# Scattering the first mixture's weighted results back to the tokens, with eight weight staging buffers in place of two

## What is computed

```python
# 1. first mixture of experts: 8 experts and 2 shared ones, 2 of the 8 for each token
topk_w, topk_idx = top_k(softmax((x @ wt.T + repeat(cond @ wg.T)) / 2), 2)   # weights divided by their sum
gp = leaky(einsum('th,ehm->etm', x, w_gate)); up = einsum('th,ehm->etm', x, w_up)
y_all = einsum('etm,emh->eth', gp * up, w_down)
y = sum over the 2 chosen experts of topk_w * y_all  +  shared(x)
# 2. attention with a relative bias over each sequence; x = x + attention(y)
# 3. a second attention, with mask, null key and normalizations
# 4. second mixture: 64 experts, 8 for each token, and a shared one; x = x + mixture(...)
```

## Time and profile before

| | us |
|---|---|
| median of 3 runs | 1968.0 (1967.81 to 1972.55) |
| the profiled execution, its own time | 1952.01 |
| its span, first to last instruction | 1950.0 |
| first mixture, to the first transfer of the attention | 0 to 307.6 |
| first attention, its slots 0 to 31 | 333.5 to about 650 |
| TensorE busy in the span | 75% |
| VectorE, ACT, GpSimd busy | 58%, 41%, 50% |

### The profile page before, as it was taken

One profiled execution on the slowest core, in us unless ns is written; L12 is line 12 of the kernel. 1 busy time (PEld: TensorE's weight loads), 2 busy tenths in 40 slices (PEclk: granted clock), 3 DMA queues, 4 the chain that ended last, 5 costly groups with the idle time before them and its releaser, 6 DMA issues. The chain is left out here.

```text
span 1950.0 us, 34468 instructions
## 1 busy us (share of the span) xinstructions
PE 1462.8 (75%) x11604; PEld 1158.4 (59%) x11605; DVE 1137.3 (58%) x2661; ACT 807.9 (41%) x1567; POOL 967.2 (50%) x888
## 2 busy tenths in 40 slices
PE   6955975576768799999999998520877877787771
PEld 4645973354445476776776776310776767676671
DVE  6633662577776546878778779630333355555555
ACT  2322431333343345655655645410444444454440
POOL 2572143665654211255555555663455555656562
PEclk9977987888889899999999999865988888888885
DMA  9553658455565000011111111636444577777755
GB/s 340 168 189 106 198 155 249 114 142 159 166 170 155 23 2 2 17 61 56 56 56 56 63 58 56 262 137 196 150 137 149 170 219 238 238 240 234 220 157 162
DMA packets 193490, 278.87 MB, mean 143 GB/s; under 512 B 27722, under 2 KB 161489, under 8 KB 190934
## 3 DMA queue, kind: packets, MB, share of 16 engines
q1 hardware_dynamic: 145030, 150.76, 26.7%
q0 software_dynamic: 33792, 84.23, 12.3%
q10 hardware_dynamic: 14544, 42.21, 6.9%
HBM read 133.38 MB, written 152.11 MB: 146 GB/s over the span
## 5 line engine op out<-in xcount | busy, mean ns | idle before, releaser
L2290 POOL DMA_INDIRECT y_rows<-se_ys,se_yidx x320 | 327.5, 1023 | 253.8 <-issue 217.1
L1461 POOL DMA_INDIRECT x_slots<-wide,a_sidx x256 | 259.6, 1014 | 85.6 <-issue 71.6
L2323 PE MATMUL ps<-se_xsT,se_up 128*128 128x128 f32 x1280 | 206.1, 329 | 93.9 <-DVE se_hT L2414 92.6
L2323 PEld LDWEIGHTS ps<-se_xsT,se_up 128*128 128x128 f32 x1280 | 194.1, 240 | 102.2 <-issue 81.4
L1450 POOL TENSOR_TENSOR flat<-flat,a_rs 128x512 f32<-128x512 f32 x64 | 69.9, 1092 | 268.3 <-DVE a_rs L1943 268.3
L2414 DVE SCALAR_TENSOR_TENSOR se_hT<-ps,se_hT 128x512 f32<-128x512 f32 x80 | 55.3, 691 | 212.1 <-ACT se_hT L2364 201.3
L2312 PE MATMUL ps<-ident,se_xs 128*128 128x128 f32 x640 | 86.3, 279 | 113.1 <-DMA se_xs<-x_slots 95.9
L2335 PE MATMUL ps<-wide,se_hT 128*128 x640 | 162.5, 399 | 1.7 <-ACT se_ys L2370 1.7
L2312 PEld LDWEIGHTS ps<-ident,se_xs 128*128 128x128 f32 x640 | 75.5, 144 | 126.7 <-issue 112.0
L2356 ACT COPY se_up<-w_up 128x256 f32 x320 | 106.9, 405 | 104.5 <-issue 100.7
L2335 PEld LDWEIGHTS ps<-wide,se_hT 128*128 128x128 f32 x640 | 125.2, 207 | 18.3 <-issue 3.3
(11 more groups left out here) (339 smaller groups left out, 3535.3 us busy)
## 6 DMA issues: line engine op xcount, KB each, us to landing
x_slots<-wide SPq DMA_DIRECT2D x40, 1032.0 KB, 13.8
se_xs<-x_slots SPq DMA_DIRECT2D x80, 516.0 KB
se_got<-y_rows ACTq DMA_DIRECT2D x64, 512.0 KB
x_slots<-wide SPq DMA_DIRECT2D x10, 1024.0 KB, 11.3
wide<-x_slots SPq DMA_DIRECT2D x20, 512.0 KB
y_slots<-wide SPq DMA_DIRECT2D x20, 512.0 KB
w_up<-in_up SPq DMA_DIRECT2D x8, 1024.0 KB
y_rows<-se_ys,se_yidx POOLq DMA_INDIRECT x320
```

Of the source, the lines that this page charges most:

```text
L1461: pool.indirect_dma_start(out=x_slots, out_offset=bass.IndirectOffsetOnAxis(ap=sidx[:, r % 2, t, k_:k_ + 1], axis=0), in_=stage[:, t, k_, ...
L2290: pool.indirect_dma_start(out=y_rows, out_offset=bass.IndirectOffsetOnAxis(ap=yidx[:, (w - 2) % TR, b:b + 1], axis=0), in_=ys[:, w % 2, b, ...
L2323: last = pe.matmul(ps[:, 2, b * P:(b + 1) * P], up[:, (w - 1) % 2, b, c, :], xsT[:, (w - 1) % 2, b, c, :], start=(c == 0), stop=(c == C - 1))
```

## The change

- Slots of the first mixture become rows of 258 numbers. `xr` holds each tile twice (one copy for each of the two experts), GpSimd writes place and weight behind the features, and scatters quarters of a half (`send`): 8 indirect DMAs, in four quarters for each half. `xr` holds two quarters, so SP loads quarter q (`load_rows`) when quarter q-2 has landed in DRAM, and all eight such loads now stand in SP's queue ahead of the first group's load.
- Evictions of a group multiply by the weight out of `xs` (two operations of 256 columns on each of ACT and VectorE where there was one of 512), and GpSimd scatters the four blocks of each group to the tokens' rows `y1_rows` (4 indirect DMAs a group, 80 in all). The store by SP, and 64 gathers, are gone.
- The rows of a group stay in `xs` until its scatter has landed; `xs` has five places, `ys` three. Group g is loaded when the scatter of group g-5 has landed.
- The two returned rows of each token are added unweighted, four tiles at a time: SP loads them (`load_returned` for the first half; one load in each of the blocks 0 to 3 of the attention for the second) and VectorE adds (two operations of 1024 columns). In the attention the adds stand in slots 4, 9, 13 and 17, and SP waits for the one before at each of its blocks.
- Staging has eight places, six of them in the part of `acc` that is written last. Eight experts load ahead of the rows of x; ACT rounds all of these before block 0 and the last two at its end; GpSimd makes all ten rests before its first scatter.
- TensorE loads ten packed words of four expert numbers once for each half (`table`) and works out the places with register arithmetic.

```diff
+        YR = 3
...
+                XS = 5
+                xs = wide[:, 0:XS * GB * ROW].rearrange("p (w b d) -> p w b d", w=XS, b=GB)
+                XR1 = 8
+                xr = sb("xr", [P, XR1, K1, ROW])
...
                     load_features(0)
-                    load_expert(0)
-                    load_expert(1)
-                    load_rows(0, 0)
-                    load_rows(0, 1)
-                    sp.wait_ge(pad_step, 1)
+                    for q in range(N1 - 2):
+                        load_expert(q)
+                    load_rows(0)
+                    load_rows(1)
+                    sp.wait_ge(pad_step, 2)
                     clear_slots(0)
+                    load_expert(N1 - 2)
+                    load_expert(N1 - 1)
                     load_features(1)
...
+                    for q in range(4, NB):
+                        load_rows(q)
                     for dst, src in ((wq, wqT), (wk, wkT), (wv, wvT), (wo, woT)):
...
                         wait(sp, t_ps, g - 1)
-                        sp.dma_start(xs[:, g % 2], xv[g // GPB][g % GPB]).then_inc(xs_in[g % 2], 16)
+                        if g >= XS:
+                            sp.wait_ge(y1_out[(g - XS) % YR], returned((g - XS) % YR, g - XS + 1))
+                        sp.dma_start(xs[:, g % XS], xv[g // GPB][g % GPB]).then_inc(xs_in[g % 2], 16)
+                    for g in range(NG1):
+                        load_slots(g)
+                        if NG1 - 4 <= g < NG1 - 2:
+                            load_returned(g - (NG1 - 4))
+                    load_returned(2)
+                    load_returned(3)
...
+                    for g in range(NG1):
+                        pool.wait_ge(ya_done, NB + g + 1)
+                        pool.wait_ge(yb_done, g + 1)
+                        for b in range(GB):
+                            pool.indirect_dma_start(
+                                out=y1_rows[g // GPB],
+                                out_offset=bass.IndirectOffsetOnAxis(ap=xs[:, g % XS, b, D:D + 1].bitcast(I32), axis=0),
+                                in_=ys[g % YR][:, b, :], in_offset=None, bounds_check=TB * P * K1 - 1, oob_is_err=False
+                                ).then_inc(y1_out[g % YR], 16)
...
+                    def table(beta):
+                        pe.wait_ge(be_ready, beta + 1)
+                        pe.load(regs[beta], be_i[0:1, beta * GPB:(beta + 1) * GPB])
...
-                            act.copy(ys[:, g % 2, 0:2, :].rearrange("p b d -> p (b d)"), ps[:, 4, :]).then_inc(ya_done, 1)
+                            for b in range(2):
+                                last = act.activation(ys[g % YR][:, b, :], ps[:, 4, b * D:(b + 1) * D], ACT.Copy,
+                                                      scale=xs[:, g % XS, b, D + 1:ROW])
...
             def sync_program(sp):
...
                     sp.dma_start(xres[:, b % 2], xv[:, b * TPB:(b + 1) * TPB, :]).then_inc(res_in[b % 2], 16)
+                    if b < 4:
+                        sp.wait_ge(added1, 4 + b)
+                        sp.dma_start(got, y1_tiles[1][:, b * TPB:(b + 1) * TPB]).then_inc(got1_in[0], 16)
                     for g in range(b * fills, (b + 1) * fills):
...
-            GATHER_AT = [2 + j + j // TPB for j in range(TB)]
+            RETURNED_AT = [4, 9, 13, 17]
```

More of the change, by code:

```diff
@@ L175, in build, with returned @@
         WIDE = 2 * C * M1 + D
[L176 to L182, removed]
+        YR = 3
+        x1_slots = [nc.dram_tensor(f"x1_slots{beta}", (EB * P, ROW), F32).ap() for beta in range(2)]
+        y1_rows = [nc.dram_tensor(f"y1_rows{beta}", (TB * P * K1, D), F32).ap() for beta in range(2)]
+        y1_tiles = [rows.rearrange("(t p k) d -> p t k d", p=P, k=K1) for rows in y1_rows]
+        y1_out = [sem(f"y1_out{w}") for w in range(YR)]
+        got1_in, added1 = [sem("got1_in0"), sem("got1_in1")], sem("added1")
+        def returned(w, groups):
+            return len(range(w, groups, YR)) * GB * 16
         def first_experts():
@@ L396, in _ @@
[L396 to L405 removed]
+                        pool.tensor_tensor(wl[:, ORDER[q], :], wf[q], wh[:, ORDER[q], :], ALU.subtract).then_inc(wl_ready, 1)
@@ L581, in _ @@
                     features(0)
-                    features(1)
                     weights(0)
                     weights(1)
+                    features(1)
+                    for q in range(2, 6):
+                        weights(q)
                     exponential(0)
+                    weights(6)
+                    weights(7)
                     for b in range(NB):
@@ L598, in _ @@
                             features(b + 2)
-                        for q in range(E1):
-                            if WEIGHTS_AT[q] == b:
-                                weights(SH1 + q)
+                        if b == 0:
+                            weights(8)
+                            weights(9)
                         if b == 4:
@@ L722, in _ @@
                     st.done(dve.memset(again[:, :, 0:1], 0.0))
-                    dve.wait_ge(made, 3)
+                    for b in range(GB):
+                        last = dve.memset(place4[:, b:b + 1], float(E1 ** b))
+                    st.done(last)
+                    dve.wait_ge(made, BLOCKS)
                     st.done(dve.tensor_copy(blk[:], blk_i[:]))
-                    dve.wait_ge(rel_in, 16)
+                    dve.wait_ge(small_in, 64)
                     for lo, hi, bucket in runs:
@@ L804, in _ @@
                             dve.wait_ge(y_ps, UNITS + g + 1)
-                            wait(dve, y1_out[g % 2], g // 2 * 16)
-                            dve.tensor_copy(ys[:, g % 2, 2:4, :].rearrange("p b d -> p (b d)"), ps[:, 5, :]).then_inc(yb_done, 1)
-                        while summed < TB and (n == NG1 + 2 or ADD_AT + 0.4 * summed <= n):
-                            add_rows(summed)
-                            summed += 1
+                            wait(dve, y1_out[g % YR], returned(g % YR, g))
+                            dve.nop(nofuse=True)
+                            for b in range(2, GB):
+                                last = dve.tensor_scalar(ys[g % YR][:, b, :], ps[:, 5, (b - 2) * D:(b - 1) * D],
+                                                         xs[:, g % XS, b, D + 1:ROW], None, ALU.mult)
+                            last.then_inc(yb_done, 1)
+                        if NG1 - 1 <= n:
+                            add_rows(n - (NG1 - 1))
         def attention1(ph, flat, later):
@@ L921, in normalize @@
                                        ALU.mult).then_inc(p_ready, 1)
-                for stored_ in y1_out:
-                    pool.wait_ge(stored_, GPB * 16)
+                for w in range(YR):
+                    pool.wait_ge(y1_out[w], returned(w, NG1))
                 keys_apart(0, 0)
@@ L946, in slot @@
                         normalize(n - 1)
-                    if n in GATHER_AT:
-                        gather(GATHER_AT.index(n))
                     if n == TPB:
```

268 lines of the change are left out of this document (129 added, 139 removed).

## The result

| | before | changed | ratio (95% interval) |
|---|---|---|---|
| median, us | 1967.9 (1959.99 to 1972.55, 4 runs) | 2019.4 (2013.84 to 2032.25, 4 runs) | 1.026 (1.023 to 1.029) |
| the profiled execution's span | 1950.0 | 2012.1 | |

The change makes the kernel 51.5 us slower. The forecast was 1981 with 1948 to 2010: the right sign and the right deciding term, but the loss four times too small, and one part of the reasoning wrong.

The account below looks back on a forecast made before the run. TensorE was busiest but only 75% of the span, so the bound changes by stage. Loss 43 us in the groups less 30 gained in the attention gave 13 us slower, 1965 profiled, 1981 us with 16 carried over; range 1948 to 2010.

Parts of the forecast that it names:

- The ring of five: First mixture: group g waits for g-5's scatter, round trip 11.75 us; two groups 19.4 us, before 11.3; loss 43 us.
- the ring doesn't bind: Rival, first mixture: round trip under 5.6 us, or gap filled by other work; 1918 us; chance 0.1.
- it binds lightly: Rival, first mixture: round trip 10.6 us, no cold clock; loss 19, gain 30, 1957 us; chance 0.2.
- Weights ahead: Around block 0: eight experts loaded early, last two behind the clearing; shared blocks end 3 us later (0 to 6).
- The shared blocks are hidden behind the second half's scatters either way: First mixture: shared blocks' delay mostly covered by scatters; their end put 3 us later (0 to 6).
- the forecast's 110: First mixture: second half's slots known at 110 us, before 105.86; first transposes at 146, 14 us later.
- No stall: First mixture, first groups: ACT goes on at about 157, not 165; register loads taken for the cause, without proof.
- the stall stays: Rival, first mixture's groups: any run of indirect DMAs delays TensorE; 20 to 50 us more, about 2015; chance 0.15.
- From group 19 to slot 0: From first mixture's end to first attention: 31 us before, equal after to within 4 us.
- The attention: First attention: 35 us gained less 5 lost, 30 us gained (11 to 40).
- SP's block 1 waits for the add: First attention: wait for slot 4's add to 369; bias landed about 396; slot 9 5 us later (0 to 12).
- Slots 9 to 24: First attention: 156 us before, 121 without the gathers and with three new adds; gain 35 us.

Follow-up runs that it names:

- Experiment 2: Changed kernel with four places in xs in place of five: 2033.2 us, 1.150 of before.
- experiment 1: Changed kernel with place and weight of each group copied out of xs by VectorE, loads waiting for no scatter: 1790.3 us, 1.014 of before.
- experiment 3: Changed kernel with the last two experts' weights loaded ahead of the rows of x and the clearing of slots: 1858.5 us, 1.052 of before.
- experiment 5: Kernel before, unchanged, profiled on a chip where before takes 1768: 1768.5 us.
- experiment 9: Changed kernel with groups 0 and 1 loaded ahead of the seventh quarter of x, 2 and 3 ahead of the eighth: 2008.5 us, 1.033 of before.
- experiment 10: Changed kernel with copied tails, last two experts' weights first, second attention's loads ahead of SP's wait, and first groups loaded early: 1936.9 us, 0.994 of before.
- experiments 4, 11, 13 and 16: Kernel before with TensorE reading ten packed words of expert numbers once for each half: 0.999, 1.001, 0.998 and 1.000 of before.
- experiments 6 and 17: Changed kernel, unchanged, on chips where before takes about 1768: 1873.0 us (1.058 of before) and 1871.8 us (1.059).
- the version of four edits: Changed kernel with copied tails, last two experts' weights first, second attention's loads before SP's wait, early first groups: 1936.9 us (0.994) and 1749.4 us (0.990).

## Why the prediction was right and wrong

**The ring of five** was forecast as the deciding term and is. Every link was there, and the sum of 11.75 us came out as 12.5. Two groups took 20.7 us, not 19.4; over seven pairs that is 9 us. In the turn shown (20.46 = 12.5 + 8.0) the round trip is 0.75 longer than the sum, and the lower clock costs 2.4 us where 2 were taken. Experiment 2 doubled the dose and experiment 1 took it away. The rivals "the ring doesn't bind" and "it binds lightly" fall. The Trainium skill, "DMA: Bandwidth & Descriptors", section on the anatomy of one DMA, gave 3.2 us for the load by an estimate. Its fit is for DMAs that GpSimd issues, and this load is SP's, on another queue; the trace has 236.50 - 232.70 = 3.8 from the issue to the transposes, between that and the 4.2 that the sum used.

**Weights ahead** is the step that failed: "The shared blocks are hidden behind the second half's scatters either way". It is the term that left its own range furthest. I saw that the last two experts stand behind the 40 blocks and that ACT waits for them, and priced it with the guess "3 us later (0 to 6)". It was 13.0: the clearing takes SP's queue 14.1 us in the kernel before and 14.8 in the changed one, and ACT's wait of 12.73 passes for the most part into blocks that I had called hidden. ACT's queue holds the hidden rows and the gates of the next block behind it. On the second chip the slots are 13.1 us later too; experiment 3 took 8.6 of these away, and where the other 4.5 come from stays open. The 13.0 moved the first group by 13.0 - 4.1 = 8.9 us more than the forecast's 110 allowed. The other 3.8 us to 158.65 came ahead of SP's last rows of x, since the second half's first scatter starts only at 122.39, 3.4 us after the slots are known, which the sum had put at nothing.

**No stall.** This was right for the changed kernel only, and its reason was wrong. I took TensorE's register loads for the cause. That could have been refuted from the trace of before, whose row for them I had not read (the sequencer's instructions of that line: ns least, median, most):

```profile
L502 PEldq TENSOR_LOAD <-e_be_i x40: 328/334/1001, 137.0 to 294.2; - x40
```

Forty loads of 0.33 us, none over 1.0, can't make 25; in experiment 5, without such waits, the same loads take 0.47 in the median and 1.15 at most. The Trainium skill, "Runtime: NRT & Kernel Launch", section on instruction fetch mechanics, gives about 200 ns for each register, and speaks against my reading as the prediction said. The trace agrees that such loads are short, and has less than the page: 0.33 us for a load of four registers, from SBUF here, where the page's figure would make 0.8. Experiments 9 and 10 have the late releases without those loads; experiments 4, 11, 13 and 16 show that packing them changes nothing (0.998 to 1.001) where there are no such waits. So the loads are not what the waits need. The rival "the stall stays" put any run of indirect DMAs down as the cause. On two chips of seven the late releases do fall in such runs, but no experiment takes the scatters away, and it did not cost the changed kernel its 20 to 50 us: its groups 0 to 19 take 181.4 us on the first chip, and 181.6 and 179.0 in experiments 6 and 17. The ring's idle time seems to cover the late releases: without the ring, in the version of four edits, groups 5 to 19 take 103.0 us on the chip of 1948 (copies at 176.48 and 279.46) and 80.3 us (161.17 and 241.49) on the chip of 1768.

**From group 19 to slot 0** I took the stretch as equal within 4 us; it is 7.4 and 7.5 us longer on the two chips, the second term outside its own range. That there are now evictions, scatters and the adds behind the last product I had set against stalls that would go. No experiment takes this term apart.

**The attention.** "SP's block 1 waits for the add" was right to the microsecond for the bias (395.7 against 396), and not by luck: on the clock of before SP goes on at 368.0 (forecast 369) and the bias is issued at 389.8 (391). But slot 9 is 10.8 us late, not 5 (505.67 - 404.98 = 100.7 us from slot 0, before 89.9). Slots 9 to 24 gained 30.2 of the 35. Together -21.5 against -30 for all slots. On the second chip the gain is 6.2 only: before's slots are 12.1 us shorter there, and the changed kernel's 3.3 longer.

**The range.** 2019 lies 9 us above it. What was missing is in the terms above: 12 to group 0, 9 in the groups, 7 before slot 0, 9 in the attention, all on the same side, 37 us, and a second mixture that fell 12 us longer in the profiled execution. No single term carries the miss. Terms that were guessed as nothing because something hides them (0 to 6, 0, 0 to 12) should each have had the full length of the wait as its far end.

**Left open.** What delays ACT's release on two of the seven chips, why the other five don't have it, and whether packing the table would shorten the wait of 25 us on the first chip: experiments 4, 11, 13 and 16 were meant to show it, but none ran on such a chip. One thing is the same in three of the waits: they end 1.3 to 4.4 us after the last scatter of a run is issued (160.54 and 164.98 in before, 156.02 and 157.32 in experiment 10, 165.82 and 168.39 in experiment 9). No run tests whether the one makes the other.

## What to carry to other kernels

When a buffer's life is stretched to the landing of what is scattered from it, write down the whole turn, from a group's last step through scatter, landing and load to the next group's transposes, and divide it by the number of groups that it lets through (here 20.5 us, for two groups with five places and for one with four). Here 128 x 2 numbers of place and weight for each block kept 128 x 258 numbers from being reused, and copying them out was worth 83 us. Price every transfer that is put behind a bulk one in a queue by the bulk one's length, and follow each engine's queue behind its wait; and put small loads that a later stage needs ahead of any wait in that queue (26 us here, fills included). The four edits, each of which undoes one such wait, turn a change that loses 5.8% into one that gains 1.0% (0.7 to 1.4) on the same kind of chip, and 0.6% (0.3 to 0.9) on the chip of 1948.

## What the hardware showed that was not expected

- Chips differ. The unchanged kernel before takes 1767 to 1769 us on five of the seven chips that the runs fell on, and 1948 and 1968 us on the two others, a factor of 1.11. The account of before between two of them, first against second: groups 0 to 19 143.5 and 107.5 us, slots 0 to 31 306.7 and 294.6, from slot 31 to the end 1309.8 and 1184.3. From the second mixture's first transposes to the end (1361.4 and 1281.9 to 1950.0 and 1771.2) it is 588.6 and 489.3, over half of the difference; this stage scatters throughout.
- On the two slower chips ACT stands idle 25.12, 17.29 and 9.24 us for products and transposes while GpSimd issues indirect DMAs back to back; the same places show 3.43, 2.76 and 2.14 us on two of the others. In before on the first chip it goes on at 164.98, though the transposes that follow the product are recorded at 143.16.
- A change's worth depends on this: 1.026 on the first chip, 1.058 and 1.059 on two others, with identical groups in the changed kernel (181.4 and 181.6 us).
